# Unread products ahead of the first maxima, and the down products of six experts by column

## The reference, cut to what matters

```python
gates = softmax(tokens @ wg); expert = argmax(gates)
pos = position of the token within its expert; keep = pos < capacity     # capacity 320
hidden = relu(x_of_expert @ w1[e] + b1[e])         # 320 x 256 by 256 x 1024
y = hidden @ w2[e] + b2[e]                         # 320 x 1024 by 1024 x 256
out = layernorm(x + gate * y)                      # rows that were dropped keep layernorm(x)
```

```python
qkv = x @ W.T + b; att = softmax(causal(q @ k.T / 4)); y = att @ v
```

## Time and profile before

| | |
|---|---|
| median of 3 runs | 1517.53 us (1507.81, 1517.53, 1519.23) |
| profiled execution | 1508.43 us, of which the profile's span is 1506.4 us |
| TensorE busy | 1421.0 us (94%) |
| VectorE, ScalarE, GpSimd busy | 982.2, 877.5, 557.6 us |
| mean granted TensorE clock | 0.975 of full speed |

### The profile page before, as it was taken

One profiled execution on the slowest core, in us unless ns is written; L12 is line 12 of the kernel. 1 busy time (PEld: TensorE's weight loads), 2 busy tenths in 40 slices (PEclk: granted clock), 3 DMA queues, 4 the chain that ended last, 5 costly groups with the idle time before them and its releaser, 6 DMA issues. The chain is left out here.

```text
span 1506.4 us, 28934 instructions
## 1 busy us (share of the span) xinstructions
PE 1421.0 (94%) x11082; PEld 1070.0 (71%) x11082; DVE 982.2 (65%) x2093; ACT 877.5 (58%) x1442; POOL 557.6 (37%) x727
## 2 busy tenths in 40 slices
PE   6998999999999999999999999998999999867997
PEld 4666666666668888888888888865655555447997
DVE  3677777767675446454544534487778989856896
ACT  1355566666556565554645546455547767637775
POOL 4146775612241121231312112152223554442766
PEclk7899999999999999999999999999999999988999
DMA  7678787755360203302021130236765643106451
GB/s 140 101 145 168 148 161 136 131 98 71 52 86 2 43 12 47 44 8 43 2 43 30 15 51 1 44 63 123 125 167 100 110 104 66 37 32 211 143 177 64
DMA packets 100343, 125.90 MB, mean 84 GB/s; under 512 B 7916, under 2 KB 90355, under 8 KB 97648
## 3 DMA queue, kind: packets, MB, share of 16 engines
q1 hardware_dynamic: 96496, 118.84, 41.2%
q0 software_dynamic: 1984, 4.09, 0.8%
q10 hardware_dynamic: 1728, 1.14, 0.3%
HBM read 50.89 MB, written 9.51 MB: 40 GB/s over the span
## 5 line engine op out<-in xcount | busy, mean ns | idle before, releaser
L954 ACT ACTIVATE probs<-eslot 128x1024 f32<-128x1024 f32 x188 | 192.4, 1023 | 103.5 <-PE eslot L690 100.4
L1176 DVE TENSOR_REDUCE mx<-mslot 128x4 f32<-128x1024 f32 x128 | 156.5, 1222 | 108.5 <-PE mslot L661 107.2
L1475 POOL TENSOR_SCALAR_AFFINE_SELECT probs<-probs 128x512 f32<-128x512 f32 x128 | 83.3, 653 | 356.0 <-ACT probs L952 355.5
L661 PE MATMUL mslot<-stack 48*128 48x256 f32 (+2 forms) x1110 | 165.2, 335 | 18.7 <-DMA stack<-split 13.0
L661 PEld LDWEIGHTS mslot<-stack 48*128 48x128 f32 (+1 forms) x1110 | 98.4, 189 | 105.7 <-issue 89.6
L1170 DVE TENSOR_REDUCE mx_blocks<-mslot 128x3 f32<-128x384 f32 x214 | 114.6, 553 | 65.6 <-PE mslot L661 50.4
L952 ACT ACTIVATE probs<-eslot 128x512 f32<-128x512 f32 (+1 forms) x256 | 111.6, 490 | 48.4 <-PE eslot L690 47.5
L705 PE MATMUL bank<-probs,v 128*32 128x256 f32 (+1 forms) x2048 | 129.0, 364 | 4.0 <-POOL probs L1475 2.3
L1414 POOL TENSOR_SCALAR ave<-amv 128x2 f32<-128x2 f32 x64 | 22.6, 353 | 297.4 <-DVE amv L1090 256.6
L690 PE MATMUL eslot<-stack 50*128 50x256 f32 (+1 forms) x1264 | 122.7, 271 | 6.6 <-ACT probs L954 3.3
L753 PE MATMUL bank<-slot_rows_sb,l 128*128 128x256 f32 x512 | 114.8, 382 | 0.0
(11 more groups left out here) (279 smaller groups left out, 3466.0 us busy)
## 6 DMA issues: line engine op xcount, KB each, us to landing
stack<-split SPq DMA_DIRECT2D x240, 256.0 KB
w<-in_w SPq DMA_DIRECT2D x16, 1024.0 KB, 6.3
slot_rows_sb<-in_proj SPq DMA_DIRECT2D x15, 256.0 KB, 5.3
slot_rows<-hTf SPq DMA_DIRECT2D x4, 650.0 KB, 4.8
slot_rows_sb<-slot_rows SPq DMA_DIRECT2D x4, 650.0 KB, 5.3
expert_rows<-slot_rows SPq DMA_DIRECT2D x8, 260.0 KB, 2.7
hT<-in_xT SPq DMA_DIRECT2D x8, 256.0 KB, 9.0
qk<-in_ctx SPq DMA_DIRECT2D x8, 256.0 KB, 3.1
```

Source lines behind the costliest of these rows:

```text
L661: mm = pe.matmul(ps[:, first:first + m], queries(u, h, k)[:, qt * P:(qt + 1) * P], keys(u, h, k)[:, 0:m], start=clear, stop=clear or qt == ...
L954: e = act.activation(PR[:, k, :, :, :].rearrange("p a k q -> p (a k q)"), ps[:, :, :, :].rearrange("p a k q -> p (a k q)"), ACT.Exp, scale ...
L1176: dve.tensor_reduce(MX[:, :, :, p].rearrange("p q a -> p a q"), MSLOT[0][:, :, :].rearrange("p a (q k) -> p a q k", q=TT), AX.X, ALU.max)\
L1475: pool.affine_select(diagonal, diagonal, [[0, 2 * TT], [1, P]], ALU.is_ge, 0.0, base=0, channel_multiplier=-1)\
```

## The change

It has two parts. Ahead of the first mask product of unit 0 TensorE makes 46 more of the unread products. For experts 1 to 6 (`BY_COLUMN`) the down products are turned: w2 is the stationary operand and the 320 tokens move, for two halves c of the channels, into the two `TURN` banks; ScalarE copies each to `down_T` (`down_high`), and TensorE transposes it back into `DOWNS` (`down_rows`, six transposes) after block f = 1 of the next expert. `combine` of these experts moves into the next expert's ups, behind f = 1, 2, 3, and all their `even` behind f = 4, 5, 6. `gated_bias(e)` of experts 1 to 6 moves from the end of expert e - 1 to behind the last up block of e; that of expert 7 stays at the end of expert 6.

```diff
--- before.py
+++ after.py
@@ -761,9 +761,13 @@
                                    start=k == 0, stop=k == 3)
             mm.then_inc(*bank_filled("down", u, e))
 
+        def unread_products(n):
+
+            for _ in range(n):
+                pe.matmul(MAXBANK[0], warm[:, 0:P], warm, start=True, stop=True)
+
         pe.wait_ge(*dve_step.at("warm"))
-        for k in range(6):
-            pe.matmul(MAXBANK[0], warm[:, 0:P], warm, start=True, stop=True)
+        unread_products(6)
         for step, u, n in ORDER:
             l = layer(u)
             if step == "T" and l > 0:
@@ -798,6 +802,8 @@
             elif step == "swap":
                 rotary_partners(u)
             elif step == "max mask":
+                if u == 0 and n == 0:
+                    unread_products(46)
                 mask_for_max(u, n)
             elif step == "exp mask":
                 mask_for_exp(u, n)
@@ -1721,6 +1727,7 @@
     hid_high, hid_low = [[both[:, k, :, :] for both in hid_both] for k in range(2)]
     xe = [sb(f"expert_rows{k}", [P, 3, WIDE]) for k in range(2)]
     eo = [sb(f"eo{k}", [P, 3, C]) for k in range(2)]
+    down_T = sb("down_T", [P, CC, CAP])
     bias = sb("gated_bias", [P, 3, C])
     st = sb("st2", [P, 3, 6])
     mv = sb("mv2", [P, 2, 3, 2])
@@ -1734,6 +1741,8 @@
     pe_rows = signal("pe_rows")
     pe_up = signal("pe_up")
     pe_down = signal("pe_down")
+    pe_down_T = signal("pe_down_T")
+    act_down_T = signal("act_down_T")
     act_rows = signal("act_rows")
     act_up = signal("act_up")
     act_high = signal("act_high")
@@ -1753,6 +1762,7 @@
     UPS = [BANK[k] for k in range(2, 5)]
     DOWNS = [BANK[k] for k in range(5, 8)]
     TURN = [BANK[k] for k in range(2)]
+    BY_COLUMN = range(1, E1 - 1)
     UP_TURNS = {1: 2, 3: 3, 5: 4, 7: 5}
     DOWN_TURNS = {(0, 3): 6, (0, 7): 7, (1, 3): 8, (1, 7): 9}
 
@@ -1809,6 +1819,31 @@
             pe.matmul(out, left[0], right[1], start=start, stop=False)
             pe.matmul(out, left[1], right[0], start=False, stop=False)
             return pe.matmul(out, left[0], right[0], start=False, stop=stop)
+
+        def down_by_column(e):
+
+            for c in range(CC):
+                cs = slice(c * P, (c + 1) * P)
+                if e - 1 in BY_COLUMN:
+                    pe.wait_ge(*act_down_T.at(e - 1, c))
+                else:
+                    pe.wait_ge(*dve_rows.at(ST // 2 - 2 + c))
+                for f in range(FC):
+                    if c == 0:
+                        pe.wait_ge(*dve_hid.at(e, f))
+                    mm = products(TURN[c][:, 0:CAP], (w2_high[e % 2][:, f, cs], w2_low[e % 2][:, f, cs]),
+                                  (hid_high[e % 2][:, f, :], hid_low[e % 2][:, f, :]), f == 0, f == FC - 1)
+                mm.then_inc(*pe_down_T(e, c))
+
+        def down_rows(e):
+
+            for c in range(CC):
+                pe.wait_ge(*act_down_T.at(e, c))
+            for j, (c0, m) in enumerate(CH):
+                pe.wait_ge(*dve_down.at(e - 1, j))
+                for c in range(CC):
+                    mm = pe.transpose(DOWNS[j][0:m, c * P:(c + 1) * P], down_T[:, c, c0:c0 + m], ident[:, :])
+                mm.then_inc(*pe_down(e, j))
 
         ups = 0
         for e in range(E1):
@@ -1826,7 +1861,12 @@
                 ups += 1
                 if e == 0 and f in UP_TURNS:
                     turn_slots(UP_TURNS[f])
+                if e - 1 in BY_COLUMN and f == 1:
+                    down_rows(e - 1)
             pe.wait_ge(*dve_low.at("w2", e))
+            if e in BY_COLUMN:
+                down_by_column(e)
+                continue
             for j, (c0, m) in enumerate(CH):
                 if e >= 1:
                     pe.wait_ge(*dve_down.at(e - 1, j))
@@ -1870,6 +1910,13 @@
             act.activation(xs_high[:, :, 2 * n * P:(2 * n + 2) * P],
                            TURN[n % 2][:, :].rearrange("p (a b) -> p a b", a=CC), ACT.Copy).then_inc(*act_rows(n))
 
+        def down_high(e, c):
+
+            act.wait_ge(*pe_down_T.at(e, c))
+            if e - 1 in BY_COLUMN:
+                act.wait_ge(*pe_down.at(e - 1, 2))
+            act.activation(down_T[:, c, :], TURN[c][:, 0:CAP], ACT.Copy).then_inc(*act_down_T(e, c))
+
         def gated_bias(e):
 
             act.wait_ge(*xe_in[e % 2].at(e))
@@ -1888,6 +1935,8 @@
         for e in range(E1):
             for f in range(FC):
                 up(e, f)
+                if e in BY_COLUMN and f == FC - 1:
+                    gated_bias(e)
                 if e == 0 and f in UP_TURNS:
                     rows_high(UP_TURNS[f])
             for n in (6, 7) if e == 0 else ():
@@ -1896,8 +1945,13 @@
                 weights_high("w1", e + 1)
                 for n in (8, 9) if e == 0 else ():
                     rows_high(n)
+                if e in BY_COLUMN:
+                    down_high(e, 0)
                 weights_high("w2", e + 1)
-                gated_bias(e + 1)
+                if e in BY_COLUMN:
+                    down_high(e, 1)
+                if e + 1 not in BY_COLUMN:
+                    gated_bias(e + 1)
 
     @block.vector
     def _(dve):
@@ -1954,8 +2008,12 @@
                                   ALU.subtract).then_inc(*dve_hid(e, f))
                 if e == 0 and f in UP_TURNS:
                     rows_low(UP_TURNS[f])
-                if e >= 1 and f in (1, 3):
+                if e == 1 and f in (1, 3):
                     even(e - 1, (f + 1) // 2)
+                if e - 1 in BY_COLUMN and f in (1, 2, 3):
+                    combine(e - 1, f - 1)
+                if e - 1 in BY_COLUMN and f in (4, 5, 6):
+                    even(e - 1, f - 4)
             if e == 0:
                 for n in (6, 7):
                     rows_low(n)
@@ -1964,6 +2022,9 @@
             if e == 0:
                 for n in (8, 9):
                     rows_low(n)
+            if e in BY_COLUMN:
+                weights_low("w2", e + 1)
+                continue
             combine(e, 0)
             if e + 1 < E1:
                 weights_low("w2", e + 1)
```

## The result

The kernel after takes 1517.87 us (median of 19 runs, 1511.05 to 1529.75), the kernel before in its 19 runs 1513.81 (1503.4 to 1521.06). The ratio is 1.005, interval 1.0029 to 1.0072: slower by 4 to 11 us. The forecast was 1514, from a change of -3.2, so the sign is wrong. That 1517.87 lies near 1514 and inside the stated range shows nothing for the forecast: its base was the median of three runs, 1517.53, and the kernel before takes 1513.81 in its 19. The profiled execution took 1527.31 us, with a span of 1525.5 and a mean granted clock of 0.971 (before 1508.43, 1506.4 and 0.975).

What follows compares the result with a forecast made beforehand. TensorE was taken as the bound: at half clock in the head, nearly without idle time in the routed part. Head -6.3 and routed +3.1 gave -3.2, put on the 1517.53 median: 1514 us, range 1500 to 1523.

Steps and rivals of the forecast that it cites:

- Products in the wait: Head: 46 unread products run from 13.76 to 23.7, inside TensorE's wait for unit 0's stack, and cost nothing.
- Clock at full level behind them: Head: clock stays full up to unit 0's maxima; unit 1's first score product comes at 42.1 instead of 47.5.
- the clock falls again: Rival, head: clock drops between unit 0's last maxima and unit 1's stack; head -1, total 1519; chance 0.17.
- Head -6.3: Head: 5.4 from unit 1's earlier first score plus 0.9 from full clock afterwards; bounds 0 and -8.
- Downs by column: Routed part: 48 turned down products take 7.04 us against 8.49 for the 72 old ones, -1.45 per expert.
- Transposes: Next expert's ups: six TensorE transposes, overlapped, cost +0.62 us per expert.
- hid 7 late: Downs of experts 2 to 6: VectorE, waiting for root 2, delays hid_low 7; TensorE waits, +0.7 each.
- add_bias 3.0 us: GpSimd during an expert's downs: add_bias runs 3.0 us from T + 4.3 to T + 7.3, then put_rows 2.
- Weights hidden with 2.7 us to spare: SyncE: w1 and w2 issued at T + 10.5 land by about T + 17.5, before ScalarE needs w2 at T + 20.2.
- weights late: Rival, experts 3 to 6: w2 lands too late; 3 us in four of them, +12, total 1526; chance 0.08.
- Expert 7: Late rows cost 3.7 in its fourth up block, hid 7 lateness 2.6, transposes 0.62: +6.9 us.
- The sum: Whole kernel: head -6.3 and routed part +3.1 make -3.2 us.

Runs made afterwards that it cites:

- products alone: Kernel before plus only the 46 unread products ahead of unit 0's first mask; ratio 0.9999.
- put_rows 2 first: Kernel after with put_rows 2 of an expert ahead of the next expert's add_bias in GpSimd's order; ratio 1.0024.
- expert 7's bias late: Kernel after with expert 7's gated_bias moved behind its last up block; ratio 1.0001.
- even 2 last: Kernel after with even 2 of the expert before moved from behind up block 6 to behind block 7; ratio 1.0078.
- all three: Kernel after with put_rows 2 ahead of add_bias, expert 7's gated_bias behind its ups and even 2 behind block 7; ratio 0.9993.
- without products: after: Kernel after without the 46 unread products; ratio 1.0074.
- without products: all three: Kernel after with put_rows 2 ahead of add_bias, expert 7's gated_bias behind its ups, even 2 behind block 7, without the 46 products; ratio 1.0003.
- without products: bias early: Kernel after without the 46 products, gated bias behind the fourth up block, add_bias ahead of put_rows 0, even 2 behind block 7; ratio 1.0096.
- products and filling, routed part of before: Kernel before plus the 46 products, two more ahead of each of unit 0's third to eighth masks, six ahead of unit 1's first; ratio 0.9971.
- products and filling, all three: The kernel "all three" plus two unread products ahead of each of unit 0's third to eighth masks and six ahead of unit 1's first; ratio 0.9959.
- products and filling, bias early: Kernel after plus filling products, gated bias behind the fourth up block, add_bias ahead of put_rows 0, even 2 behind block 7; ratio 1.0016.
- products and filling, GpSimd's order: "products and filling, all three" with GpSimd's order changed: roots 0 to 2, put_rows 0, add_bias, put_rows 1 and 2; ratio 0.9949, 1502.71 us.

## Why the prediction went wrong, point by point

The step that failed is the length of `add_bias`, put at 3.0 us and measured at up to 5.25 in its new place, with what hangs on it: put_rows 2, the rows and weights queued behind it, and expert 7's wait. The head's gain was too large as well. The points below take the terms one by one.

All runs in one table. The last column is what the ratio leaves once the routed part's own difference is taken off: (ratio - 1) x 1513 less (slots to end - 148.3). It stands for the head.

| kernel | ratio | slots to end, us | rest for the head, us |
|---|---|---|---|
| after | 1.0050 | 161.3 | -5.4 |
| products alone | 0.9999 | 148.4 | -0.3 |
| put_rows 2 first | 1.0024 | 156.1 | -4.2 |
| expert 7's bias late | 1.0001 | 153.9 | -5.4 |
| even 2 last | 1.0078 | 165.8 | -5.7 |
| all three | 0.9993 | 148.8 | -1.6 |
| without products: after | 1.0074 | 160.1 | -0.6 |
| without products: all three | 1.0003 | 148.4 | +0.4 |
| without products: bias early | 1.0096 | 156.3 | +6.5 |
| products and filling, routed part of before | 0.9971 | 148.1 | -4.2 |
| products and filling, all three | 0.9959 | 148.4 | -6.3 |
| products and filling, bias early | 1.0016 | 156.6 | -5.9 |
| products and filling, GpSimd's order | 0.9949 | 145.7 | -5.1 |

A single entry is uncertain by some 5 us, as its ratio is (0.0035 of 1513). The means are -3.8 for the six with the 46 products, -5.4 for the four with the filling ones, and +2.1 for the three without. The three without have the head of before and should give 0, which shows how far such a mean can be off. The entry of "even 2 last" counts the 3.1 us in expert 0 as routed part; without them it is -2.6.

The profiles give a second reading. The issue of `w<-in_up`, some 70 us from the start, is at 75.7 in before and at 72.6 to 73.0 in the three without products (mean of the four 73.5), at 70.1 to 74.2 in the six with the 46 (mean 72.1), and at 69.0 to 71.1 in the four with the filling ones (mean 70.1): -1.5 and -3.4.

- **Products in the wait: right.** 14.82 to 24.9 against 13.76 to 23.7; they began 1.1 later because the products ahead of them did, and two masks and a wait of 0.67 follow.
- **Clock at full level behind them: wrong, the rival "the clock falls again".** It fell at 34.4 (in the products alone at about 43.7, 0.87 in 25 to 50), and unit 1's first score came at 43.39 against 42.1; in the other five kernels with the 46 products alone it came at 41.5 to 42.4, behind a wait for the stack. The rival put the head at -1 in this case. Against before's own profile 4.1 us were kept, the ratios give a mean of -3.8 and the mean of four profiles -1.5, so the rival's figure is not excluded. With the clock held the forecast's 42.1 holds (42.05 and 41.52).
- **Head -6.3: too large.** The base of 47.51 was that of a profile with a long half clock; three others with the same head have 44.1 to 44.5. Even with the clock held the head is worth 3.4 to 5.4 us by the two readings.
- **Downs by column, 7.12 us against 7.04: right.** So is expert 1's interval, -2.55 against -1.45 - 1.7 + 0.62 = -2.53: the saving, the stall of the earlier trace rows gone, the transposes paid.
- **Transposes: right.** Six records in 0.82, from 1409.59; the next up product at 1410.16, 0.57 behind the first transpose. The forecast's 0.62 holds. By the Trainium skill's page "TensorE: Matmul & The Clock Gate", section "Part 4: PE-mode transpose", counted one behind the other, it would have been 1.65; this trace doesn't agree with that count.
- **hid 7 late: right in kind, 1.14 to 1.26 instead of 0.7.** But it isn't a price of its own in this kernel: taken away, the stretch from expert 1's downs to TensorE's end was as long as with it (118.1 against 117.3). It absorbed part of a lateness that another chain makes, and it is the limit once that lateness is gone (downs 16.2 to 16.6 apart with put_rows 2 first, 14.7 to 15.6 with all three edits). Step and rivals treated waits as terms that add up.
- **add_bias 3.0 us: the step that failed.** The forecast took the duration from the earlier trace rows, a place where VectorE's `w_low` began at 1446.4, behind the addition's end at 1445.2, and moved the instruction to one where both `w_low` lie beside it. It measured 5.25 (twice), 4.17 and 4.19, and 2.12 the one time that no `w_low` was beside it. In expert 6, 2.25 of put_rows 2's lateness (T + 10.85 for 7.4) is this length, 1.1 stood in GpSimd's queue ahead of it. In expert 5, with 2.12, put_rows 2 came at T + 7.6, as forecast. Behind it `slot_rows` was issued at T + 13.0 to 15.5 (9.6) and w1 and w2 from T + 13.9 to T + 16.4 (10.5), expert 5 apart. That this order costs the time is shown: with put_rows 2 ahead of `add_bias` slots to end is 5.3 less.
- **Weights hidden with 2.7 us to spare: wrong.** Lateness of 3.4 to 5.9 us used the spare up: waits of 0.41, 0.41 and 1.76 at the start of the ups of experts 4, 5 and 6. The rival "weights late" came true, in small: 2.6 us in three places against its 12.
- **Expert 7: right in kind, too small.** From expert 6's downs to expert 7's the forecast has -1.45 + 0.7 + 3.7 + 0.62 = +3.6, measured +8.92: 0.56 of the difference is the wait for hid 7, 2.5 the wait in the fourth block (6.20 for 3.7), and by difference 2.3 the half clock of 1500 to 1505, which wasn't in the sum at all. In its own downs the wait for hid 7 is 0.95 for 2.6, and they cost +1.19.
- **The sum.** Routed +13.1 for +3.1. Of the 10.0 between them the intervals from expert 2's downs to expert 6's carry 6.1 (+0.53, +1.16, +1.35, +2.50 for -0.13 each), the next 5.3, and the last downs -1.4. Head -1.5 to -4 for -6.3. On the level: the profiled execution of before was one of its faster ones, so the forecast's base, the median of three, was no better known than 1508 to 1519; the medians of 19 runs are 1513.8 and 1517.9, and the sign was decided by the routed part.

What stays open: why the clock falls where it does in the attention part, and how much the 46 products alone win (0.3 to 5.7 us by the single runs, 1.5 by the mean of the profiles).

## What to carry to other kernels

When an instruction is moved, its duration has to be taken from what will run beside it at the new place, and what is queued behind it followed round: here an addition on GpSimd that takes 2.1 us undisturbed, and 2.6 to 3.2 at its old place, took 5.25 at the new one, and the DMA issue queued behind it set the pitch of the loop. A wait of the bounding engine is only worth removing when it isn't the slack of a longer chain; removing one first and looking where it comes back tells that cheaply. And where two engines disturb each other, an order in which the short one goes first can be worth trying: here it gave 2.8 us, though what came to stand beside the long one grew in its turn. Last, the profile that a forecast starts from is one execution: 5.4 us of this one's forecast were measured from a stretch that took 3 us less in three other profiles of the same head.

## What was not expected of the hardware

- GpSimd's addition of three 256-column pieces takes 2.10 to 2.15 us by itself, 3.9 to 5.5 beside VectorE's subtraction of 2048 columns; issuing an indirect DMA takes 0.92 to 1.7 without it and up to 3.2 beside it. In the kernel before the addition took 2.61 to 3.16 with no `w_low` beside it, but narrow subtractions. VectorE's own instruction grows too, from 2.28 to 2.59 beside the additions of 5.25 and to as much as 3.24 beside that of 4.17. The Trainium skill, page "SBUF — State Buffer", section "Who interferes with whom", says that a VectorE instruction with two inputs in SBUF and a GpSimd instruction that reads SBUF exclude each other for a whole instruction, and whichever starts second waits. The lengthened additions agree with that in kind: 1.8 to 3.4 us are added beside one or two `w_low` of 2.3 us and more. The same section infers that a two-input VectorE instruction doesn't hold up the making of DMA descriptors. The indirect DMAs here were held up beside it; as they also take their row numbers from SBUF, these runs don't tell whether it is that reading or the descriptors.
- The granted clock fell in stretches where TensorE was busy nearly all the time (71 us of 75, clock 0.86 to 0.91), and differently in each execution of kernels with the same work there. The end of the attention part differed by up to 14 us (1353.1 to 1367.3) between profiles, more than the head accounts for.
- In the same head, without the added products, the clock of 25 to 50 was 0.52, 0.71, 0.82 and 0.83 in four profiles, with the 46 products 0.73 to 0.93 in six, and with the filling ones 1.00 in all four.
